# The rest of q and k in the linear stage: a product of the negative identity and a ScalarE copy, in place of a VectorE subtraction

## What is computed

```
h = layernorm(x) * (1 + ca) + sa
x = x + ga * linear_attention(h)            # 16 heads of 8, causal, then a layer norm
h = layernorm(x) * (1 + cb) + sb
x = x + gb * ffn(h)                         # softmax attention, then 8 experts, one chosen per token

# inside ffn, 32 batches of 128 tokens in the original, here 8 of 512:
q, k, v = layernorm(h) @ w_qkv
attn = softmax(q @ k.T / sqrt(8));  y = attn @ v;  h = h + y @ w_proj
h = h + expert[argmax(layernorm(h) @ gate_w + gate_b)](layernorm(h))
```

## Time and profile before

| | |
|---|---|
| median of 3 runs | 689.78 us |
| the profiled execution | 690.73 us |
| its span, first to last instruction | 688.9 us |
| busy: TensorE, VectorE, ScalarE, GpSimd | 89%, 85%, 73%, 60% |
| mean granted TensorE clock | 0.971 |

### The profile page before, as it was taken

How to read it: one execution, slowest core, us unless ns; L and a number is a source line. 1 busy time by engine, 2 the same in 40 slices (tenths; PEclk the granted TensorE clock), 3 DMA queues, 4 the chain that set the end, 5 groups by cost and what they waited for, 6 DMA issues and landing times.

```text
span 688.9 us, 16395 instructions
## 1 busy us (share of the span) xinstructions
PE 615.9 (89%) x5313; PEld 308.2 (45%) x5313; DVE 586.3 (85%) x1481; ACT 503.4 (73%) x1079; POOL 414.9 (60%) x931
## 2 busy tenths in 40 slices
PE   4688789988877898899999999999999999899994
PEld 3355556665544222223233232332323322589993
DVE  6886999998877988899999999999999994776552
ACT  3653777788655378888888888888888889755661
POOL 4411567667655743436676887887877862566553
PEclk9998999999999589999999999999999999999998
DMA  6564143335354121137120301203012010456510
GB/s 182 154 236 131 38 131 125 121 126 184 115 162 139 47 92 47 47 97 240 35 61 2 116 25 48 81 13 116 24 41 89 13 47 22 141 172 182 159 34 9
DMA packets 42899, 66.25 MB, mean 96 GB/s; under 512 B 7948, under 2 KB 36335, under 8 KB 39808
## 3 DMA queue, kind: packets, MB, share of 16 engines
q1 hardware_dynamic: 39232, 56.73, 27.8%
q0 software_dynamic: 3296, 8.41, 3.4%
q10 hardware_dynamic: 288, 0.07, 0.0%
HBM read 41.64 MB, written 22.26 MB: 93 GB/s over the span
## 4 chain that ended last, share of the span: by engine, by line
PE 53%; ACT 20%; DVE 11%; issue 6%; SPq 5%; POOL 3%; DMA 2%; ACTq 0%; POOLq 0%; DVEq 0%
PE bank L1118 12%; ACT arena L2082 10%; PE pair L1107 8%; PE bank L1079 7%; PE pair L1366 4%; DVE arena L1619 3%; DVE arena L1437 2%; PE bank L1129 2%; PE pair L1375 2%; PE bank L1375 2%; ACT arena L2051 2%; PE pair L1159 2%; PE bank L960 1%; PE pair L1079 1%; POOL arena L683 1%
## 5 line engine op out<-in xcount | busy, mean ns | idle before, releaser
L2082 ACT ACTIVATE arena<-pair 128x512 f32<-128x512 f32 x506 | 278.1, 603 | 52.6 <-PE pair L1107 50.6
L1619 DVE TENSOR_REDUCE arena<-bank 128x1 f32<-128x512 f32 x388 | 251.4, 682 | 10.1 <-PE bank L1079 7.1
L1107 PE MATMUL pair<-q_stack,k_stack 64*128 64x512 bf16 x506 | 158.1, 386 | 5.9 <-ACT arena L2082 5.1
L1079 PE MATMUL bank<-k_stack,q_stack 63*128 63x512 bf16 x388 | 136.6, 396 | 8.9 <-DVE arena L1619 4.8
L1118 PE MATMUL bank<-arena,values 128*9 128x512 f32 x1024 | 134.5, 597 | 1.6 <-ACT arena L2082 1.5
L1437 DVE TENSOR_TENSOR arena<-bank,cst 128x512 f32<-128x512 f32 x128 | 82.0, 682 | 16.5 <-PE bank L946 16.1
L1619 DVE TENSOR_REDUCE arena<-pair 128x1 f32<-128x512 f32 x124 | 84.3, 680 | 2.4 <-PE pair L1079 2.0
L748 POOL TENSOR_TENSOR arena<-arena 128x32 f32<-128x32 f32 (+6 forms) x312 | 68.4, 219 | 24.4
L1079 PEld LDWEIGHTS bank<-k_stack,q_stack 63*128 63x128 bf16 x388 | 33.1, 93 | 110.1 <-ACT arena L2087 24.8
L1107 PEld LDWEIGHTS pair<-q_stack,k_stack 64*128 64x128 bf16 x506 | 40.6, 93 | 47.4 <-ACT arena L2082 21.4
L1079 PE MATMUL pair<-k_stack,q_stack 63*128 63x512 bf16 x124 | 49.0, 395 | 0.5 <-ACT arena L2103 0.3
(11 more groups left out here) (318 smaller groups left out, 1222.1 us busy)
## 6 DMA issues: line engine op xcount, KB each, us to landing
softmax_parts<-arena SPq DMA_DIRECT2D x8, 768.0 KB, 4.1
q_stack<-softmax_parts SPq DMA_DIRECT2D x48, 128.0 KB
k_stack<-softmax_parts SPq DMA_DIRECT2D x48, 128.0 KB
linear_parts<-arena SPq DMA_DIRECT2D x7, 768.0 KB, 3.7
q_stack<-linear_parts SPq DMA_DIRECT2D x42, 128.0 KB
k_stack<-linear_parts SPq DMA_DIRECT2D x42, 128.0 KB
arena<-in_L_ffn_w_dram SPq DMA_DIRECT2D x16, 256.0 KB, 4.4
v_all<-token_rows SPq DMA_DIRECT2D x20, 192.5 KB, 2.8
```

The costliest lines, as they stand in the source:

```text
L1079: pe.matmul(bank[:], qs[b % 2][rows, slot, qt * P:(qt + 1) * P], ks[b % 2][rows, slot, :], start=True, stop=True).then_inc(d_s_m, 1)
L1107: pe.matmul(score_bank(s)[:], ks[u][rows, 2 * g + x, kt * P:(kt + 1) * P], qs[u][rows, 2 * g + x, :], start=True, stop=True).then_inc(d_s_ ...
L1619: dve.reduce_max(mx[:, m % 2, col:col + 1], bank[:], AX).then_inc(d_s_mr, 1)
L2082: act.activation(pt[:, kt % 2, x, half, :], score_bank(s)[:], ACT.Exp, scale=SCALE).then_inc(d_s_e, 1)
```

## The change

In steps 3 to 8 the rest r1 = value - p1 of q and k is formed in PSUM: TensorE multiplies p1 (bf16, 128x512) by the negative identity and adds the product to the bank that holds the value, and ScalarE copies the bank to c_r1. VectorE's subtraction is gone. The product for z = 0 stands right behind c_key at d = 0, that for z = 1 right behind c_value at d = 1. On ScalarE the copy for z = 0 stands behind c_first_part(b, 1) at d = 0, that for z = 1 at d = 1 between values and c_normed. GpSimd makes the negative identity once, in the setup. Semaphores that nothing used are dropped, which issues no instruction.

```
+        k.minus = sb("minus_identity", [P, P], BF16)
...
+        c_s_rp = sem_early("c_rest_products")
...
                                 pool.tensor_scalar(center, k.ident, -1.0 / D, None, ALU.add).then_inc(w_s_ct, 1)
+                                pool.tensor_scalar(k.minus[:], k.ident, -1.0, None, ALU.mult).then_inc(w_s_ct, 1)
...
+                def c_rest_product(b, z):
+                    if b == 0 and z == 0:
+                        pe.wait_ge(w_s_ct, 2)
+                    pe.wait_ge(c_s_p1, 2 * b + z + 1)
+                    pe.matmul((b_x, b_z)[z][:], k.minus[:], c_parts[:, 3 * z, :], start=False, stop=True,
+                              skip_group_check=True).then_inc(c_s_rp, 1)
...
                         if d == 0 and has(s - 3):
                             c_key(s - 3)
+                            c_rest_product(s - 3, 0)
                         if d == 1 and has(s - 3):
                             c_value(s - 3)
+                            c_rest_product(s - 3, 1)
...
-                def c_rest(b, z):
-                    dve.wait_ge(c_s_p1, 2 * b + z + 1)
-                    wait(dve, c_s_p3, 2 * b + z - 1)
-                    dve.tensor_tensor(c_r1[:, z, :], (b_x, b_z)[z][:], c_parts[:, 3 * z, :], ALU.subtract
-                                      ).then_inc(c_s_r1, 1)
...
-                            if has(s - 3):
-                                c_rest(s - 3, 0)
                             if has(s - 2):
                                 c_variances(s - 2, 1)
-                        if d == 1 and has(s - 3):
-                            c_rest(s - 3, 1)
...
+                def c_rest(b, z):
+                    act.wait_ge(c_s_rp, 2 * b + z + 1)
+                    wait(act, c_s_p3, 2 * b + z - 1)
+                    act.activation(c_r1[:, z, :], (b_x, b_z)[z][:], ACT.Copy).then_inc(c_s_r1, 1)
...
                                 c_first_part(s - 3, 1)
+                                c_rest(s - 3, 0)
                         if d == 1:
                             if has(s + 1):
                                 values(s + 1)
+                            if has(s - 3):
+                                c_rest(s - 3, 1)
                             if has(s - 2):
                                 c_normed(s - 2, 1)
```

More of the change, by code:

```diff
@@ L359, in program @@
         s_y, s_yc = sem_early("b_projected"), sem_early("b_projected_out")
-        c_s_st = [sem_early(f"c_stats{m}") for m in range(3)]
-        c_s_mv = [sem_early(f"c_means{m}") for m in range(3)]
+        c_s_st = [None] + [sem_early(f"c_stats{m}") for m in (1, 2)]
+        c_s_mv = [None] + [sem_early(f"c_means{m}") for m in (1, 2)]
         c_s_ve = [sem_early(f"c_variances{m}") for m in range(3)]
         c_s_rs = [sem_early(f"c_rstd{m}") for m in range(3)]
-        c_s_nm = [sem_early(f"c_mean_turned{m}") for m in range(3)]
-        c_s_nb = [sem_early(f"c_shift{m}") for m in range(3)]
+        c_s_nm = [None] + [sem_early(f"c_mean_turned{m}") for m in (1, 2)]
+        c_s_nb = [None] + [sem_early(f"c_shift{m}") for m in (1, 2)]
         c_s_n = [sem_early(f"c_normed{m}") for m in range(3)]
```

## The result

The changed kernel takes 692.63 us (median of 5 runs, 692.1 to 692.95); the kernel before, run beside it, 689.78 us (5 runs, 688.19 to 690.97). The ratio is 1.0041, 95% interval 1.0025 to 1.0057: it is slower, by 2.8 us. The forecast was 692.2.

What follows compares the result with a forecast made beforehand. Bound: the chain of waits through VectorE's sums, GpSimd, ScalarE's c_normed and TensorE. Losses 1.26 (steps 3 to 5) + 0.85 (6, 7) + 0.33 (8) = 2.44 us, so 692.2 us; case bounds 691.5 to 693.8, full range 688.9 to 694.8.

Steps and rivals of the forecast that it cites:

- the first sum: Steps 3 to 8: VectorE's q subtraction leaves the chain of waits, 6 x 0.59 = 3.5 us gained.
- TensorE's cost: 12 added products, 0.38 us each, successor 0.22 later; q's covered in steps 3, 4, 5, 7, costing 0.22 in 6 and 8.
- ScalarE's cost: 12 added copies from PSUM, 0.48 us of the engine each; q's copy covered by 1.50 us idle before c_normed.
- The new wait: ScalarE's k copy waits for the k product behind c_value: c_normed 0.42 us later, 1.26 us over steps 3 to 5.
- Step 6: TensorE has no gap before the turn; c_normed at 178.03 against 177.96, +0.07 us.
- step 7: c_normed +1.32 us from the late k product, less 0.47 by the earlier store; +0.85 together with Step 6.
- if the transfer doesn't follow: Steps 6 and 7 if the softmax parts' store does not come 0.6 us earlier: 1.39 us lost, not 0.85.
- Step 8: q and k products delay the fifth score product, so VectorE waits for TensorE: +0.33 us; late c_normed just covered.
- A: Rival: k product early enough, c_normed follows VectorE, the relief wins; about -1.2 us, 688.6; chance 0.15.
- B: Rival: granted clock, one low stretch more (+1.3 us, 693.5, chance 0.09) or fewer (-1.3 us, 690.9, chance 0.08).
- C: Rival: product usable after 0.22 not 0.38 us, c_value hands over sooner; 1.2 us lost, 691.0; chance 0.10.
- D: Rival: product replaces the bank's content instead of adding to it; same time, so no price and no chance given.

Runs made afterwards that it cites:

- e3: Changed kernel with the k rest back on VectorE, only q by product and copy; 702.0 against 703.11 us for the kernel before, ratio 0.9987.
- e2: Changed kernel with the q rest back on VectorE, only k by product and copy; 707.02 against 703.11 us for the kernel before, ratio 1.0056.
- e6: The changed kernel again, unedited, on the chip of the experiments; 708.7 against 705.97 us for the kernel before, ratio 1.0042.
- e1: Changed kernel with the k product ahead of c_value on TensorE, not behind it; 703.58 against 703.11 us for the kernel before, ratio 1.0006.
- e7: Changed kernel with the k product one place later on TensorE, behind a_turn; 709.44 against 705.97 us for the kernel before, ratio 1.0061.
- first pair: The measurement's two profiled executions, kernel before and changed kernel; +2.25 us from the turn of step 3 to c_normed of batch 7.
- e5: The kernel before again, unedited, on the chip of the experiments; 705.43 us in its one run.
- second pair: The profiled executions of e5 and e6, the same two kernels once more; +2.39 us from the turn of step 3 to c_normed of batch 7.
- e9: The kernel of e3 measured again, unedited; 702.62 against 705.21 us for the kernel before, ratio 0.9965.
- e4: Changed kernel with ScalarE's k copy behind c_normed, not ahead of it; 706.05 against 703.11 us for the kernel before, ratio 1.0043.
- e8: Kernel before with VectorE's q subtraction moved behind c_variances, nothing added elsewhere; 705.35 against 705.97 us for the kernel before, ratio 0.9998.

## Why the prediction was right

The forecast was 692.2 us, within 691.5 to 693.8 for this case; measured 692.63. By its steps:

**The view it started from.** It set the chain of waits above the busy shares and then asked what is late next. Both were needed: the first sum from the chain alone, 3.5 us gained, has the wrong sign, and e3 shows that even a clean relief brings 0.3 and not 0.6 us in a full step.

**TensorE's cost.** Forecast: 0.38 us for the product, its successor 0.22 later, as L1030. Measured: 0.38, and 129.50 to 129.72, 0.22. q's product costs 0.22 in steps 6 and 8 (in step 6, 174.24 to 174.45 is 0.21) and nothing in 3, 4, 5 and 7, where the turn waited anyway. The Trainium skill (TensorE: Matmul & The Clock Gate, Back-to-back issue gap) has about 131 ns for such a slot in a sustained stream and about 216 ns for one that stands alone; the rows here fit the second.

**ScalarE's cost.** Forecast 0.48 us a copy from the spacing in the earlier trace rows; measured 0.48 (127.86 to 128.34) and 0.49 (129.92 to 130.41). Its full 0.59 would have been too much.

**The new wait.** Forecast for c_normed of step 4: 3.85 us behind the turn (130.98 - 127.13). Measured 3.84. The hand-over was 0.04 and not 0.05. The full step was forecast at 24.1 and is 24.10 in after, e2 and e6. That the place of the product sets it, e1 and e7 show; that q has no part in the loss, e2 and e3.

**Steps 6 and 7.** Step 6 was forecast at +0.07; turn 3 to c_normed of step 6 came out at +1.25 and +1.19 for 1.33. In step 7 the two pairs part. ScalarE in that step:

```profile
195.56 0.60 ACT L2068 ACTIVATE arena<-pair 128x512 bf16<-128x512 f32 x1 [3.49 <-DMA softmax_parts<-arena]
...
200.14 0.60 ACT L2073 ACTIVATE arena<-pair 128x512 f32<-128x512 f32 x1 [1.98 <-PE pair L1070]
200.63 1.63 ACT L2053 ACTIVATE arena<-x_all,arena 128x128 f32<-128x128 f32 x4
```

The forecast had the store, and with it L2068, 0.6 us earlier by its GpSimd part. In the first pair that did not come: L2068 stands 17.32 us behind c_normed of step 6, before 17.22. On SP's queue one of the stack loads ahead of the store took longer than its like in before (1.13 us at 188.34):

```profile
188.08 1.67 SPq L224 DMA_DIRECT2D k_stack<-linear_parts  x1
```

The twelve loads began 0.53 us earlier behind c_normed of step 6, as forecast, and the 0.54 us more of this one used that up: the store was issued at 191.06, 12.82 us behind c_normed, before at 190.77, 12.81. Step 7 cost 1.32 us, the price given for "if the transfer doesn't follow". In e6 the store was issued at 188.36, L2068 stands 16.71 us behind c_normed (17.31 in e5), and the step cost 0.71, for 0.78 forecast. So the mechanism was right, and whether it comes depends on the queue of that execution. The prediction said that c_normed would be more than 3.9 us behind the turn in step 7; it is 3.84 (196.79 to 200.63), since the k product follows c_value's start by 0.89 us and not by the 0.99 at which the next product stood before.

**Step 8.** VectorE and TensorE there (L1625 the maxima, L1089 the score product, before L1619 and L1079):

```profile
223.56 4.93 DVE L1625 TENSOR_REDUCE arena<-bank 128x1 f32<-128x512 f32 x8 [0.63 <-PE bank L1089]
```

```profile
222.83 0.38 PE L1070 MATMUL pair<-arena,minus_identity 128*128 128x512 bf16 x1
223.14 0.39 PE L1089 MATMUL bank<-k_stack,q_stack 63*128 63x512 bf16 x2
```

VectorE waits 0.63 us for the score product. From c_key to the fifth maximum it is 5.89 us (217.67 to 223.56), before 5.57 (217.03 to 222.60): +0.32 for 0.33. The cover for the late c_normed held, but by little: GpSimd ends the new h at 228.06 (226.79 + 1.27), VectorE asks for it at 228.41.

But of these 0.32 us the part behind the turn, 0.11, did not last in the first pair. The eight maxima took 4.93 us and not the 5.06 of the earlier trace rows, where TensorE's clock fell about 1 us later in the step (granted clock 0.95 from the turn to VectorE's next normalise, before 0.90), and VectorE's next normalise starts 9.67 us behind the turn, before 9.69; in the second pair it starts 9.81 behind it and 9.68. The +0.43 of the table's last row is therefore the clock alone, and of the +0.32 of the second pair 0.13 is the k product, near the 0.11 forecast.

**The rivals.** A (the relief wins, 688.6) is what e1 makes true, and its price for a full step holds: 0.06 us forecast, 0.09 measured; e3 gains 0.30 because TensorE is also spared the k product's 0.22. Its 0.6 and 0.3 us for steps 7 and 8 don't come in e1. In step 7 the k copy still sets c_normed, 2.95 us behind the turn (195.97 to 198.92), where before it is 2.62 (196.41 to 199.03), and from the turn of step 3 to c_normed of batch 7 e1 takes 146.83 us (103.12 to 249.95), e5 146.11. So even A's condition would not have made the whole change faster. B (the clock) did occur and with both signs: in step 7 -0.9 us in the first pair and +1.9 us in e2, and behind the turn of step 8 +0.2 to +0.4 us in the pairs, which no term had. C (half of it) is out: the copy waited for the whole 0.38 us of the product. D had no price of its own, and no time could tell it from the forecast.

**The sum.** 2.44 us forecast for the stretch, 2.25 and 2.39 measured; 2.8 (1.7 to 3.9) by the timed runs. That the first pair comes so near is in part luck: step 7 without the store's help cost 0.54 us more than forecast and the last row of the table, where the clock came in, 0.3 more, and the shifted stretch of low clock in step 7 gave 0.9 back. The second pair, with no low stretch in step 7 and the store's help in it, is the one that bears out the terms: +1.19, +0.71 and +0.49 for 1.33, 0.78 and 0.33, with 0.20 of the last from the clock.

**What stays open.** Why e2's timed loss is 3.9 and not 2.6 us is settled only in part: its trace and the clocks of its runs point at the granted clock. Nor do the runs show what makes a load on SP's queue take 1.13 or 1.67 us, or when a stretch of low clock comes in step 7. The best version found is e3, q alone: 0.9987 (0.9974 to 1.0) and, as e9, 0.9965 (0.9946 to 0.9985) of the kernel before, where the change is at 1.0041.

## What to carry to other kernels

When work is taken off an engine that stands in the chain of waits, put the start of what replaces it beside the time at which the chain needed the old result: here the copy could not start before c_value's end plus one product, 0.42 us too late, and everything behind it on an in-order engine paid for that, though every engine's share looked better. Of two like edits (q and k) test each alone: one had cover and gained 0.3 us a step, the other cost 0.4. And where an operation waits at the head of a queue, move its producer forward (e1, which took the loss away and no more), not the waiting operation back (e4), which only hands the wait to the next user of its buffer.

## What the runs showed of the hardware that was not expected

**VectorE and GpSimd hold each other up.** L1607 (two operands in SBUF) ends 0.55 us behind GpSimd's L698, whether it starts 0.94 us before that end (e8, 121.62 and 122.56) or 0.67 (before, 122.13 and 122.80). A small instruction shows it more plainly. VectorE's addition of a constant to 128x4 takes 0.17 us in step 8 of after (L1490); in step 3 it stands like this, and GpSimd beside it:

```profile
108.21 1.10 DVE L1490 TENSOR_SCALAR arena<-arena 128x4 f32<-128x4 f32 x1
...
229.72 0.17 DVE L1490 TENSOR_SCALAR arena<-arena 128x4 f32<-128x4 f32 x1
```

```profile
108.02 1.27 POOL L705 TENSOR_TENSOR arena<-arena 128x512 f32<-128x512 f32 x1 [1.53 <-ACT arena L2053]
```

It takes 1.10 us at 108.21 and ends at 109.31, 0.02 behind GpSimd's 109.29. The Trainium skill (SBUF — State Buffer, SBUF: two separate sides) states that GpSimd and VectorE share a pair of ports, which VectorE uses for an instruction in a two-port mode or with two inputs in SBUF, and that the first to start holds it for the whole instruction while the other waits in full. The traces agree, with 0.17 us grown to 1.10. Such meetings also took back some of VectorE's relief: L1490's 14 instructions of these steps take 4.2 us in after, L1478's 2.4 in before. So a VectorE instruction moved earlier by half a microsecond may gain nothing, or lose, by what GpSimd does just then.

**The price of a stretch of low clock depends on where it falls.** In step 7 two stretches with the same mean clock of the window (0.89) cost 1.5 us in before and 0.55 in after. In before the low stretch lies behind the last turn of the step (granted clock 0.72 from 211.81 to 217.89), where TensorE is busy throughout: 6.08 us for what takes 4.58 at 2.4 GHz in e5. In after it lies behind the second turn (0.67 from 203.41 to 208.52), where TensorE is busy for only 3.0 of 4.4 us at 2.4 GHz in e6: 5.11 us for 4.38, and the part behind it gets 0.17 us back.

**The same kernel took 2% more in the runs of the experiments,** 703 to 706 us and not 690, though its full steps are equal (23.72 and 23.71 us). A good part of the difference lies late in the kernel: in e5 TensorE waits 4.82 us at 616.57 and 5.61 us at 635.53, and the granted clock from 600 to 650 us is 0.86; in the measurement's profile of before TensorE waits for nothing longer than 0.7 us behind 595 us, and that clock is 1.00. What causes these waits is not shown.
